# Attention scores as three products of first parts and rests, rests taken by VectorE, and an earlier final normalisation, in a one-core decoder layer

## The reference, cut to what matters

```python
x = x + local_attention(layernorm(x))          # 8 heads, blocks of 12 with 12 past positions
x = x + cross_attention(layernorm(x), context)
x = x + expert_mixture(layernorm(x))           # 12 experts, top 3, three routers
```

```python
lat = layer_norm(latents) ; ctx = layer_norm(context)
q = (lat @ Wq) ; k, v = split(ctx @ Wkv) ; k = apply_rope(k, cos, sin)
attn = softmax(clip(einsum('bhnd,bhsd->bhns', q, k) * scale, -11, 11))
out = (einsum('bhns,bhsd->bhnd', attn, v)) @ Wo + bo
```

## Time and profile before

| what | us |
|---|---|
| three runs | 454.59, 455.76, 459.03 |
| their median | 455.76 |
| the profiled execution | 457.88 |
| its span, first to last instruction | 456.1 |
| PE busy / DVE busy / POOL busy / ACT busy | 422.6 / 340.6 / 244.4 / 196.3 |
| mean granted clock of TensorE, as a share of 2.4 GHz | 0.988 |

### The profile page before, as it was taken

One profiled execution on the slowest core, in us unless ns is written; L12 is line 12 of the kernel. 1 busy time (PEld: TensorE's weight loads), 2 busy tenths in 40 slices (PEclk: granted clock), 3 DMA queues, 4 the chain that ended last, 5 costly groups with the idle time before them and its releaser, 6 DMA issues.

```text
span 456.1 us, 8468 instructions
## 1 busy us (share of the span) xinstructions
PE 422.6 (93%) x3168; PEld 310.3 (68%) x3168; DVE 340.6 (75%) x700; ACT 196.3 (43%) x312; POOL 244.4 (54%) x217
## 2 busy tenths in 40 slices
PE   3997789999999999998996998979989999999996
PEld 2666666666766766666764676748767788888885
DVE  8788658979997577987665688797985993654554
ACT  7758363664555353554234544423546543200000
POOL 5757248996898768885963664563432442000000
PEclk9999999999999999999997999989999999999999
DMA  7675414000000000000000000424627660000000
GB/s 181 170 162 82 88 23 79 0 1 1 0 2 1 1 1 1 0 1 2 0 2 1 1 1 0 142 47 69 140 46 191 118 133 1 6 6 11 8 6 13
DMA packets 75434, 19.85 MB, mean 44 GB/s; under 512 B 66741, under 2 KB 73834, under 8 KB 75394
## 3 DMA queue, kind: packets, MB, share of 16 engines
q1 hardware_dynamic: 72628, 18.27, 18.9%
q10 hardware_dynamic: 2766, 1.04, 1.0%
HBM read 17.27 MB, written 2.02 MB: 42 GB/s over the span
## 4 chain that ended last, share of the span: by engine, by line
PE 71%; DVE 12%; SPq 5%; issue 5%; ACT 4%; POOL 2%; DMA 1%; DVEq 0%; ACTq 0%; POOLq 0%
PE psum L1162 11%; PE psum L1145 9%; PE psum L955 8%; PE psum L1343 5%; PE psum L1344 5%; PE psum L1342 5%; PE psum L1306 4%; PE psum L1308 4%; PE psum L1307 4%; PE psum L1181 3%; SPq L375 3%; PE psum L1172 3%; PE psum L1064 3%; ACT e_sb L781 2%; DVE rden L1566 1%
## 5 line engine op out<-in xcount | busy, mean ns | idle before, releaser
L528 POOL TENSOR_TENSOR e_part<-e_sb 128x512 f32<-128x512 f32 x64 | 88.8, 1403 | 49.6 <-DVE e_sb L1559 37.6
L781 ACT ACTIVATE e_sb<-psum 128x1024 f32<-128x1024 f32 x64 | 62.2, 1022 | 20.9 <-PE psum L1145 20.9
L1162 PE MATMUL psum<-e_sb,v_sb 128*64 128x256 f32 x512 | 64.0, 391 | 0.8 <-ACT v_sb L688 0.8
L1145 PE MATMUL psum<-q_t,kT 64*128 64x256 f32 x512 | 64.2, 389 | 0.0
L1761 DVE SCALAR_TENSOR_TENSOR x_sb<-psum,dw,x_sb 128x128 f32<-128x128 f32 x96 | 33.7, 351 | 36.9 <-PE psum L1344 34.3
L1559 DVE TENSOR_SCALAR e_sb<-e_sb 128x1024 f32<-128x1024 f32 x64 | 54.7, 888 | 5.4 <-ACT e_sb L781 5.3
L1566 DVE RECIPROCAL rden<-psum 128x256 f32<-128x256 f32 x32 | 55.8, 1744 | 0.3
L760 ACT ACTIVATE kT<-psum 128x512 f32<-128x512 f32 x32 | 19.1, 598 | 85.6 <-PE psum L1064 85.3
L1145 PEld LDWEIGHTS psum<-q_t,kT 64*128 64x128 f32 x512 | 46.7, 186 | 9.6 <-issue 5.0
L568 POOL TENSOR_TENSOR xeT_lo<-xeT,xeT_hi 128x512 fp32r<-128x512 f32 x24 | 30.8, 1289 | 40.5 <-ACT xeT_hi L795 38.0
L520 POOL TENSOR_TENSOR k_rot<-rope_a,rope_b 128x512 f32<-128x512 f32 x32 | 42.2, 1319 | 18.5 <-DVE rope_b L1446 18.5
(11 more groups left out here) (194 smaller groups left out, 773.6 us busy)
## 6 DMA issues: line engine op xcount, KB each, us to landing
w_raw<-in_L_ffn_W_dram SPq DMA_DIRECT2D x96, 64.0 KB, 2.3
gates<-gate_dram SPq DMA_DIRECT2D x6, 768.0 KB, 4.4
ctx_sb<-in_ctx_dram SPq DMA_DIRECT2D x4, 256.0 KB, 6.1
vbd<-v_dram SPq DMA_DIRECT2D x16, 52.6 KB
v_dram<-v_tok SPq DMA_DIRECT2D x4, 136.0 KB, 3.6
raw<-in_L_xattn_Wkv_dram SPq DMA_DIRECT2D x2, 256.0 KB, 5.2
k_rot<-in_L_xattn_Wkv_dram SPq DMA_DIRECT2D x2, 256.0 KB, 4.4
k_rot<-in_L_xattn_Wq_dram SPq DMA_DIRECT2D x2, 256.0 KB, 5.6
```

What stands on the lines that cost most here:

```text
L528: pool.tensor_tensor(e_part[:, p % 2, half, :, :], e_sb[:, i % ERING, :, 0, :], e_sb[:, i % ERING, :, 1, :], ALU.add)\
L781: act.activation(e_sb[:, i % ERING, :, :, :].rearrange("p a k t -> p (a k t)"), psum[:, a:a + 2, :].rearrange("p a b -> p (a b)"), ACT.Exp ...
L1145: mm = pe.matmul(psum[:, 2 * (i % 2) + a, t * S:(t + 1) * S], kT[rows, p % 3, kt * P:(kt + 1) * P], q_t[rows, j % 2, p % 2, :], start=True ...
L1162: mm = pe.matmul(psum[DX * a:DX * a + DX, pv_bank(p), 0:S], v_sb[g % 2][:, kt, 2 * pp + a, :], e_sb[:, i % ERING, a, t, :], start=(kt == 0 ...
```

## The change

- The copies of keys and queries out of bank 6 by ACT are written as float32r (`kT_hi`, `q_hi`), and raise a new semaphore `misc_hi_done`.
- DVE then subtracts the copy from what is still in bank 6 and writes the rest as float32r (`keys_lo`, `queries_lo`, 32 and 16 times, 128x512 each); this, and no longer ACT's copy, raises `misc_read`.
- Each score product becomes three float32r products into the same place: first part by first part, key first part by query rest, key rest by query first part.
- In round 22 `rstd_of(LN_F, ...)` moves ahead of the three adds of POOL, `final_norm(0, 1)` ahead of the rotation on DVE, and `final_normalize(0)` ahead of the key copy on ACT.
- Buffers are laid out anew.

```diff
--- before.py
+++ after.py
@@ -213,13 +213,17 @@
         lat_hi = sb("lat_hi", [P, B * S], F32R, second)
         lat_lo = sb("lat_lo", [P, B * S], F32R, second)
 
-        q_t = sb("q_t", [P, 2, QH // 2, S], F32, second)
-        kT = sb("kT", [P, 3, SC], F32, second)
+        q_hi = sb("q_hi", [P, 2, QH // 2, S], F32R, second)
+        kT_hi = sb("kT_hi", [P, 3, SC], F32R, second)
         e_sb = sb("e_sb", [P, ERING, 2, KH, S], F32, second)
         v_sb.append(sb("v_sb1", [P, KC, HG, DX], F32, second))
-        e_part = sb("e_part", [P, 2, 2, 2, S], F32, second)
+        sb("awT_rest", [P, 16], F32, second)
+        kT_lo = sb("kT_lo", [P, 2, SC], F32R, second)
+        q_lo = sb("q_lo", [P, 2, QH // 2, S], F32R, second)
         rden = sb("rden", [P, 2, S], F32, second)
         o_t = sb("o_t", [P, 2, PPB, S], F32, second)
+        sb("below", [P, 7144], F32, second)
+        e_part = sb("e_part", [P, 2, 2, 2, S], F32, second)
         second.close()
         cross.close()
 
@@ -269,7 +273,7 @@
-            ... k_rot_done misc_ps misc_read score_ps exp_done
+            ... k_rot_done misc_hi_done misc_ps misc_read score_ps exp_done
@@ -323,6 +327,7 @@
             if r + 3 < NPAIR:
                 MISC.append(("keys", r + 3))
         MISC_NO = {what: n for n, what in enumerate(MISC)}
+        HI_NO = {what: n for n, what in enumerate(w for w in MISC if w[0] in ("keys", "queries"))}
 
         def pv_bank(p):
 
@@ -578,12 +583,12 @@
                     for part in range(2):
                         if r == rounds[part]:
                             rstd_of(LN_1 + (2 * b + part) * TPB, TPB)
+                if r == NORM_ROUND:
+                    rstd_of(LN_F, NT // 2)
                 if r + 1 < NPAIR:
                     weights_summed(2 * r + 2)
                     weights_summed(2 * r + 3)
                     halves_summed(r + 1)
-                if r == NORM_ROUND:
-                    rstd_of(LN_F, NT // 2)
                 if r in ROUND_KEYS:
                     key_sum(r + K_LEAD)
                 if r == FILLED:
@@ -757,7 +762,7 @@
                 misc_wait(("keys", p))
                 if p >= 3:
                     act.wait_ge(s["score_ps"], 2 * (p - 2))
-                act.activation(kT[:, p % 3, :], bank(MISC_BANK), ACT.Copy).then_inc(s["misc_read"], 1)
+                act.activation(kT_hi[:, p % 3, :], bank(MISC_BANK), ACT.Copy).then_inc(s["misc_hi_done"], 1)
 
             outputs_turned(2)
             keys_turned(0)
@@ -770,7 +775,7 @@
                 misc_wait(("queries", j))
                 if j >= 2:
                     act.wait_ge(s["score_ps"], QH * (j - 1))
-                act.activation(q_t[:, j % 2, :, :], bank(MISC_BANK).rearrange("p (a t) -> p a t", t=S), ACT.Copy).then_inc(s["misc_read"], 1)
+                act.activation(q_hi[:, j % 2, :, :], bank(MISC_BANK).rearrange("p (a t) -> p a t", t=S), ACT.Copy).then_inc(s["misc_hi_done"], 1)
 
             def exponent(i):
                 act.wait_ge(s["score_ps"], i + 1)
@@ -864,14 +869,14 @@
                 if r % 2 == 0 and r // 2 + 1 < NQ:
                     queries_out(r // 2 + 1)
                 route_1(2 * r)
+                if r == NORM_ROUND:
+                    final_normalize(0)
                 if r in extras and extras[r][0] == "latents":
                     misc_wait(extras[r])
                     latents_f(extras[r][1])
                 if r + 3 < NPAIR:
                     keys_turned(r + 3)
                 route_1(2 * r + 1)
-                if r == NORM_ROUND:
-                    final_normalize(0)
                 if r == NPAIR - 2:
                     act.wait_ge(s["unit_ps"], len(UNIT))
                     act.wait_ge(s["k_rot_done"], NG * KC)
@@ -1142,8 +1147,11 @@
                     kt = KH * half + t
                     for a in range(2):
                         rows = slice(DX * a, DX * a + DX)
-                        mm = pe.matmul(psum[:, 2 * (i % 2) + a, t * S:(t + 1) * S], kT[rows, p % 3, kt * P:(kt + 1) * P],
-                                       q_t[rows, j % 2, p % 2, :], start=True, stop=True)
+                        o = psum[:, 2 * (i % 2) + a, t * S:(t + 1) * S]
+                        hi, lo = kT_hi[rows, p % 3, kt * P:(kt + 1) * P], kT_lo[rows, p % 2, kt * P:(kt + 1) * P]
+                        pe.matmul(o, hi, q_hi[rows, j % 2, p % 2, :], start=True, stop=False)
+                        pe.matmul(o, hi, q_lo[rows, j % 2, p % 2, :], start=False, stop=False)
+                        mm = pe.matmul(o, lo, q_hi[rows, j % 2, p % 2, :], start=False, stop=True)
                 mm.then_inc(s["score_ps"], 1)
 
             def weigh_values(i):
@@ -1544,11 +1552,26 @@
             latents(0, 1)
             local_normalize(3)
             latents(0, 2)
+            def keys_lo(p):
+                dve.wait_ge(s["misc_hi_done"], HI_NO["keys", p] + 1)
+                if p >= 2:
+                    dve.wait_ge(s["score_ps"], 2 * (p - 1))
+                dve.tensor_tensor(kT_lo[:, p % 2, :], bank(MISC_BANK), kT_hi[:, p % 3, :].bitcast(F32), ALU.subtract).then_inc(s["misc_read"], 1)
+
+            def queries_lo(j):
+                dve.wait_ge(s["misc_hi_done"], HI_NO["queries", j] + 1)
+                if j >= 2:
+                    dve.wait_ge(s["score_ps"], QH * (j - 1))
+                dve.tensor_tensor(q_lo[:, j % 2, :, :], bank(MISC_BANK).rearrange("p (a t) -> p a t", t=S),
+                                  q_hi[:, j % 2, :, :].bitcast(F32), ALU.subtract).then_inc(s["misc_read"], 1)
+
             local_residual(1)
+            keys_lo(0)
             latents_lo(0)
             context_normalize(1)
             for b in range(2, B):
                 context_offset(b)
+            queries_lo(0)
             local_normalize(4)
             local_normalize(5)
 
@@ -1673,7 +1696,9 @@
                        .then_inc(s["h_lo_done"], 1)
 
             clip(0)
+            keys_lo(1)
             clip(1)
+            keys_lo(2)
             local_residual(2)
             local_residual(3)
             key_unit(10)
@@ -1701,8 +1726,12 @@
                 if r + 1 < NPAIR:
                     clip(2 * r + 2)
                     clip(2 * r + 3)
+                if r == NORM_ROUND:
+                    final_norm(0, 1)
                 if r in CONTEXT_ROUND:
                     context_lo(CONTEXT_ROUND[r])
+                if r % 2 == 0 and r // 2 + 1 < NQ:
+                    queries_lo(r // 2 + 1)
                 if r in beside:
                     work, arg = beside[r]
                     work(arg)
@@ -1714,8 +1743,8 @@
                         add_projected(extras[r])
                 if r in ROUND_KEYS:
                     key_unit(ROUND_KEYS[r])
-                if r == NORM_ROUND:
-                    final_norm(0, 1)
+                if r + 3 < NPAIR:
+                    keys_lo(r + 3)
                 route_1(2 * r + 1)
                 if r == NPAIR - 2:
                     turn_weights(0)
```

More of the change, by code:

```diff
@@ L271, in decoder_layer @@
             ct_ps ctx_f_done ctx_hi_done ctx_lo_done unit_ps rope_done v_done
-            xn1_done lat_in_done lat_ps lat_f_done lat_hi_done lat_lo_done bo_added             k_rot_done misc_ps misc_read score_ps exp_done
+            xn1_done lat_in_done lat_ps lat_f_done lat_hi_done lat_lo_done bo_added             k_rot_done misc_hi_done misc_ps misc_read score_ps exp_done
             clip_done part_done es_done pv_ps den_ps rden_done ox_done tail_ps x2_done ld_w0 ld_w1 ld_w2 ld_w3
```

## The result

The changed kernel takes 461.37 us (median of 4, 460.23 to 463.18), the kernel before 455.67 beside it (454.59 to 459.03): ratio 1.0114, 95% interval 1.0077 to 1.0151. It is slower, outside the range of 442 to 459. The profiled execution of after took 462.21 us, its span is 460.3.

A forecast was written before the change was run, and what follows sets the result against it. PE sets the pace, with DVE close behind. The terms 0 + 2.0 - 1.3 + 0.3 - 1.0 - 0.8 - 0.4 - 5.1 = -6.3 us gave 449.5 from the median of 455.76, rounded to 450; range 442 to 459.

The forecast's parts named there:

- Scores: Score products on PE: 24 records in 12 pairs take 1.68 us, 0.32 less per round, 10.2 us where PE is the bound.
- scores slower: Rival for PE's scores: matmuls start in program order, 0.27 us more per round, 461 in all; chance 0.08.
- Rests: On DVE: 48 subtractions from PSUM at 0.68 us each add 32.6 us, to be hidden by DVE's slack.
- The term that I called the least sure: Rounds 1 to 10: of 7.8 us that DVE waits for POOL in clips and bias adds, 3.0 would go.
- Rounds 1 to 10: Stretch of 70.71 us where DVE becomes the bound: +2.0 us, ends -3.2 and +5.0.
- 15 to 19: Stretch of 37.83 us, DVE's work with rests 37.6, even on the whole: +0.3 us, ends -1.6 and +1.5.
- Bank 6 is held until the rest is taken: PE asks for bank 6 again over 2 us later, so this wait got nothing; DVE's lateness would be no additional one.
- The normalisation: Earlier normalisation of the first half: PE's stall in round 23 falls from 5.42 to 1.8 us, -3.6; with the clock -5.1.
- The clock's share of -1.5: Round 23: with a stall of 1.8 us the clock should not fall, so 3.4 us at half clock become 1.7.
- DVE takes all of it: Rival: rests cost their full 0.68 in rounds 1 to 10 and 15 to 19; 454.6 us, up to 458; chance 0.25.
- All the bad ends together: Sum of every stretch's and the normalisation's unfavourable end: +2.5 us, giving 460 and 458.
- PE's gain came in full: Rival: DVE's waiting for POOL shrinks by most of 7.8 us, about -14, so 442; chance 0.17. Sign: rotation wait stays 4.2.

The follow-up runs named there:

- heads_alternate: The changed kernel with the three score products of the two heads taken in turn instead of three of one head, then three of the other; 460.27 us.
- rests_unused: The changed kernel with all 48 rests still taken, but float32 scores of the first parts alone, so the rests go into no product; 461.53 us.
- order_fix: The changed kernel with the output bias spread over rounds 11 to 14, 20 and 21, and the queries' rest ahead of the third latents part and the offset; 456.09 us.
- rests_small: The changed kernel with only 16 of 512 columns of each rest subtracted from the third on, all semaphores and products kept; 451.11 us.
- norm_only: The kernel before with only the earlier normalisation of round 22, scores left in float32; 452.87 us.
- scores_only: The changed kernel with the three normalisation moves of round 22 undone; 466.11 us.
- unheld: The changed kernel with ACT first copying bank 6 whole into its own buffer and releasing it, first parts and rests then made from that copy; 479.76 us.
- norm_bias: The kernel before with the earlier normalisation of round 22 and the output bias spread one tile at a time over eight rounds, scores float32; 451.53 us.

## Why the prediction was wrong, point by point

**Scores.** Right: pairs formed, 1.41 us between the outer starts, plain odd rounds went from 6.45 to 6.14 us (0.31 where 0.32 was forecast). The time of 461 that the rival "scores slower" gave agrees with the result by accident; its mechanism is refuted by the records and by heads_alternate. Pairs formed though three products of one head stand before three of the other, as the rows of line 971 had let me expect.

**Rests.** Size right (0.685 and 0.683). The term that I called the least sure, how much of DVE's waiting for POOL goes in rounds 1 to 10, erred on the careful side: I took 3.0 us, and the clips alone became 5.4 shorter there (18.32 to 12.90 us). The bias adds stayed as they were, three of four at 1.35 to 1.38. So DVE is busy 69.44 us in these rounds, less than their length before, and by that sum alone nothing would have been lost there.

**Stretches: this failed.** Rounds 1 to 10 were put at +2.0 (ends -3.2 and +5.0) and came out at +7.4; 15 to 19 at +0.3 and came out at +2.9; 20 to 22 at -1.0 and came out at +1.7. Three things stand behind it.

First, the stretch of ten rounds was treated as one store of slack: 65.55 of 70.71 us busy, so 5 us of room. In fact 4.4 us of it lay in rounds 3, 4, 9 and 10 (2.7 and 1.7), 0.5 in 5 and 6, and 0.14 in each of the pairs 1-2 and 7-8. Rounds 1-2 grew by 1.6 and 7-8 by 1.05, although the clips shrank. rests_unused shows it most plainly. Half of the growth, 3.7 us, came in rounds 5 and 6, where the averages had half a microsecond of room: the turn of the context waits 3.11 us for a rest behind the bias, and the clock falls behind that. order_fix, which moves the bias, has 14.44 us there. The buffers between the engines are one or two deep, so room in round 3 can't help round 2.

Second, the step "Bank 6 is held until the rest is taken ... I give that wait nothing while DVE is on time; if DVE is late, it is the same lateness, not another". It looked at DVE's backlog only at the end of a round. In the middle, behind latents and clips, the subtraction is late every time these are there, and PE, which before waited for ACT alone, waits 10.3 us for rests in after. rests_small prices this order at 4.6 us or more with subtractions of next to no length; this is a difference of single profiled executions.

Third, the clock. I excluded a fall because waits of up to 1.4 us had left none. Six waits of PE ahead of round 23 now last 1.55 to 3.1 us, and three spells of 3.4 us at 1.2 GHz follow some of them; each costs about half its length, 1.7 us, in rounds 3-4, 5-6 and 19-20, some 5 us together. Without them the change would be about level with before (+5.7 less 5.1, an estimate that leaves before its own spell): still without the gain forecast.

Rounds 11 to 14 (-1.1, forecast -1.3), 24 to 28 (-0.7, forecast -0.8) and 29 and 30 (-0.5, forecast -0.4) were right: there PE was the bound and stayed it.

**The normalisation.** The stall fell to 2.03 us in norm_only, forecast 1.8, and rounds 23 and 24 are 3.3 us shorter (22.27 to 18.98; forecast -3.6 for the stall). The clock's share of -1.5 did not come there: the clock still falls for 3.4 us after the wait. With the scores part the offset delays a rest, and the stall is paid in round 22 as 2.27 us. Forecast -5.1 in all; measured -3.8 alone; from scores_only to after -4.7 by the medians and -3.5 by the ratios.

**The chances.** The rival "DVE takes all of it", up to 458, was the right direction, but even it gave 5.0 for rounds 1 to 10 as the worst: it counted only DVE's busy time and added no wait and no clock. A wait which the change adds had no term with a bad end of its own. All the bad ends together gave 458, and this came out 3 us above them. The text calls round 23 the only one that pays in this rival, but its sum also counts 2.3 us from rounds 11 to 14 and 20 to 22.

**The signs.** Two of those I named spoke against each other. Rounds 1 to 10 took 78.1 us, over the 75 named for "DVE takes it all". The value unit's wait for the rotation went only from 4.2 to 5.5, which by my words would have meant that PE's gain came in full. It was no sign of that, since most of the new waiting, 10.3 us, stands at bank 6, where I had looked for none.

## What to carry to other kernels

Read the slack of the engine that takes on work in stretches no longer than the buffers between it and its users allow, here one or two rounds; an average over ten rounds hides those in which it is full. When the release of a shared bank moves from one engine to another, the new wait is everything that stands ahead of the releasing instruction in its queue, and it counts even if the instruction itself costs nothing. Before trading one engine's time for another's, make the other's time bigger without the gain (rests_unused): if the total is the same as with it, the gain is worth nothing there. Then look at single rounds too, since here a gain of 3 us was hidden by a clock that fell in one of the two kernels.

## What the runs showed of the hardware

A subtraction 128x512 takes 0.67 to 0.69 us from PSUM, beside a busy POOL too, in each of the six kernels that take all rests from there. From a copy in SBUF it takes 0.98 and 1.43 us in the mean. An instruction of DVE that is held up by an add of POOL ends at a fixed distance behind the end of that add: the clips and the subtractions from SBUF 0.55 us (16 of 16 long clips in before, 24 of 24 long subtractions in unheld), the bias adds 0.15 us (6 of the 8 in before).

After a wait of PE of about 2 us the clock sometimes falls and sometimes not. In after, the wait of 2.32 us that ends at 213.35 is followed by 3.4 us at 1.2 GHz from 213.9, and the one of 2.27 us that ends at 245.34 by nothing. norm_only waits 2.03 us at the turn and falls, norm_bias waits 2.04 there and stays at full clock. What decides between them these runs don't show. It does mean that one wait more or less can move a total by 1.7 us beyond its own length, so differences of 2 us between single executions are read here only where stretches agree.
